# The first product of the routed expert tiles, issued in two halves of 64 tokens

## The reference: what is computed

```python
x = x + gnn(layernorm(x), adj, adj)           # adjacency normalized, two large products
h = layernorm(layernorm(x)) * gamma + beta    # (the second one inside the ffn)
sw1, sw2, ew1, ew2 = (bit_quant(w) for w in ...)   # each row: round(w / scale) in {-1, 0, 1}, times scale
shared = silu(h @ sw1.T) @ sw2.T                          # 512 -> 1024 -> 512
probs = softmax(h @ router_w.T); e = argmax(probs); gate = max(probs)
routed = gate * (silu(h @ ew1[e].T) @ ew2[e].T)           # only the expert that is chosen
out = x + shared + routed
```

## Time and profile before

| | |
|---|---|
| median of three runs | 705.73 us (703.64 to 707.68) |
| the profiled execution's own time | 702.86 us |
| its span, first to last instruction | 701.2 us |
| TensorE matmuls busy, share of the span | 648.4 us, 92% |
| TensorE weight loads busy | 381.6 us, 54% |
| DVE busy | 469.2 us, 67% |
| ACT busy | 389.6 us, 56% |
| mean granted TensorE clock | 0.991 |

### The profile page before, as it was taken

The page is one execution under the profiler, slowest core; times in us unless marked ns, Lnnn a source line. Parts: engine busy times, 40 slices in busy tenths (PEclk is TensorE's granted clock), DMA queues, the critical chain, the costliest instruction groups (busy, mean ns, idle before and its releaser), DMA issues.

```text
span 701.2 us, 15954 instructions
## 1 busy us (share of the span) xinstructions
PE 648.4 (92%) x5281; PEld 381.6 (54%) x5281; DVE 469.2 (67%) x1031; ACT 389.6 (56%) x726; POOL 151.7 (22%) x171
## 2 busy tenths in 40 slices
PE   0798999999979999999998789999999999999995
PEld 0343444444434554445434367777767677777773
DVE  4878988566664555688788669756855565555553
ACT  1658648879986776777657653333432242424241
POOL 2234430000000000012323206200021353434322
PEclk9999999999999999999999999999999999999999
DMA  8999962675897777866576896643284876868641
GB/s 348 417 421 417 421 255 62 194 196 155 237 242 251 264 259 253 282 225 237 175 270 218 241 248 166 173 111 96 76 141 131 197 195 176 187 185 181 177 141 31
DMA packets 107103, 151.68 MB, mean 216 GB/s; under 512 B 64286, under 2 KB 64286, under 8 KB 102944
## 3 DMA queue, kind: packets, MB, share of 16 engines
q1 hardware_dynamic: 91280, 117.74, 53.5%
q0 software_dynamic: 6960, 20.99, 9.9%
q10 hardware_dynamic: 8800, 12.09, 5.7%
HBM read 119.57 MB, written 19.16 MB: 198 GB/s over the span
## 4 chain that ended last, share of the span: by engine, by line
PE 54%; DMA 14%; DVE 13%; ACT 9%; issue 7%; SPq 1%; POOL 1%; DVEq 0%; ACTq 0%; POOLq 0%
PE bank L1545 16%; PE bank L1517 16%; PE bank L1390 7%; PE bank L1392 7%; PE bank L1391 7%; DMA region<-in_adj_t 6%; ACT junk L748 4%; DMA work<-in_w 3%; ACT region L760 2%; DVE work L1096 2%; DVE region L986 2%; PE bank L1421 2%; DMA work<-in_adj_t 1%; DVE region L1192 1%; DVE region L982 1%
## 5 line engine op out<-in xcount | busy, mean ns | idle before, releaser
L1545 PE MATMUL bank<-region,work 128*128 (+1 forms) x624 | 141.6, 379 | 4.4 <-DVE work L1244 4.2
L886 ACT ACTIVATE work<-work 128x512 f32<-128x512 f32 x78 | 48.5, 622 | 171.1 <-DVE work L1234 171.1
L1390 PE MATMUL bank<-zreg,work 128*128 (+1 forms) x256 | 98.2, 384 | 12.3 <-DVE work L1164 10.9
L1517 PE MATMUL bank<-zreg,region 128*128 128x128 f16 x1728 | 100.9, 219 | 0.0
L1517 PEld LDWEIGHTS bank<-zreg,region 128*128 (+1 forms) x1728 | 98.1, 98 | 4.2
L1391 PE MATMUL bank<-zreg,work 128*128 (+1 forms) x256 | 98.2, 384 | 0.0
L1392 PE MATMUL bank<-zreg,work 128*128 (+1 forms) x256 | 98.0, 383 | 0.0
L1390 PE MATMUL bank<-region,work 128*128 128x512 f16 x192 | 74.1, 386 | 25.4 <-DVE region L1010 25.4
L1545 PEld LDWEIGHTS bank<-region,work 128*128 128x128 f16 x624 | 58.9, 98 | 70.4 <-issue 7.4
L748 ACT ACTIVATE junk<-work 128x512 f16<-128x512 f32 x124 | 77.6, 625 | 15.9 <-DMA work<-in_w 13.8
L1244 DVE SCALAR_TENSOR_TENSOR work<-work 128x512 f16<-128x512 f32 x78 | 53.7, 691 | 48.8 <-ACT work L893 48.8
(11 more groups left out here) (154 smaller groups left out, 946.8 us busy)
## 6 DMA issues: line engine op xcount, KB each, us to landing
work<-in_w SPq DMA_DIRECT2D x62, 512.0 KB, 4.1
region<-in_adj SPq DMA_DIRECT2D x16, 1024.0 KB, 10.7
region<-in_adj_t SPq DMA_DIRECT2D x16, 1024.0 KB, 7.5
work<-in_adj_t SPq DMA_DIRECT2D x32, 384.0 KB, 4.4
zreg<-s_scratch SPq DMA_DIRECT2D x24, 256.0 KB, 3.9
xb<-in_w SPq DMA_DIRECT2D x10, 512.0 KB, 4.2
zreg<-in_x SPq DMA_DIRECT2D x4, 1024.0 KB, 9.7
h_scratch<-hb POOLq DMA_DIRECT2D x16, 256.0 KB, 3.4
```

The source lines that it names most:

```text
L886: nc.scalar.activation(h1[:, cols], pre[:, cols], ACT.Silu).then_inc(h1_ok, 1)
L1390: nc.tensor.matmul(dst, a_hi, b_hi, start=start, stop=False, skip_group_check=True)
L1517: last = nc.tensor.matmul(ps_h[b][f // 4][:, (f % 4) * P:(f % 4 + 1) * P], w, ht[n % RING][:, c:c + P], start=(f % 4 == 0 and d == 0 and h ...
L1545: last = nc.tensor.matmul(ps_y[b][:, :].rearrange("p (d c) -> p d c", d=DB), h1hl[:, b, h, f * P:(f + 1) * P], w, start=(f == 0 and h == 0 ...
```

## The change

For tiles from `NT` on, the 128 tokens are taken in two halves of 64 columns: for each weight square the first half's high and low part, then the second half's, so four matmuls, each with its own weight load, where there were two. `w` is still written once per square, ahead of the loops. The shared tiles keep one pass of 128 columns. The `start` flag stays on the first matmul of a bank.

```diff
                 for f in range(FB):
                     for d in range(DB):
                         w = w1t[:, ds(u * (4 * CHUNK) + (f // 2) * CHUNK + d * 2 * P + (f % 2) * P, P)]
-                        for h in range(2):
-                            c = (h * DB + d) * P
-                            last = nc.tensor.matmul(ps_h[b][f // 4][:, (f % 4) * P:(f % 4 + 1) * P], w,
-                                                    ht[n % RING][:, c:c + P], start=(f % 4 == 0 and d == 0 and h == 0),
-                                                    stop=False, skip_group_check=True)
+                        width = P if n < NT else P // 2
+                        for t in range(0, P, width):
+                            for h in range(2):
+                                c = (h * DB + d) * P + t
+                                last = nc.tensor.matmul(ps_h[b][f // 4][:, (f % 4) * P + t:(f % 4) * P + t + width], w,
+                                                        ht[n % RING][:, c:c + width],
+                                                        start=(f % 4 == 0 and d == 0 and h == 0 and t == 0),
+                                                        stop=False, skip_group_check=True)
                 last.then_inc(m1_ok, 1)
```

## The result

The changed kernel took 744.54 us (median of 4 runs, 743.23 to 745.34) beside 706.7 us for the kernel before: a ratio of 1.0546, 95% interval 1.0516 to 1.0577, **+38 us**. The forecast was +17, with 742 as the upper end of the range. The same kernel, run again on two later occasions beside the kernel before, took 721.21 us (ratio 1.0278, 1.0228 to 1.0327) and 721.99 us (1.0253, 1.0212 to 1.0294), **+19 us** each, while the kernel before took 701.92 and 702.74. The sign is the same each time, and the loss lies in the routed tiles each time, but 19 us of the first measurement belong to that occasion. Both parts have to be explained.

A forecast was written before the change was run, and what follows sets the result against it. TensorE was taken to bound the routed tiles: 0.80 us for the first product plus 0.03 for the second, times 23, is 19.1 us, less 1.8 hidden, +17.3 on 705.73, giving 723.0 us; 8-in-10 range 709 to 742.

The forecast's parts named there:

- TensorE bounds the stage: Routed tiles: TensorE sets the end, at 7.03 us a tile without idle time, so any lengthening is paid 23 times.
- The array: First product: matmuls of 64 columns cost TensorE's array 29.2 ns each, +0.16 us a tile, 3.6 us over 23 tiles.
- One address per square: First product of routed tiles: still one run-time address computation per weight square, 736 records in all.
- A queue of 32 instructions: Start of a first product: 32 queued instructions now hold four weight squares instead of eight, a lead of 0.47 us.
- The stream's step: TensorE's instruction stream, first product: 132 + 12 + 7 = 151 ns a square, against 117 for the array.
- 1.8 us hidden behind the chain at the first routed tiles: First routed tiles: TensorE's wait behind a gather, a scales transfer and DVE work absorbs 1.8 us of the loss.
- The read of the expert's number: Second product, two blocks in: stream needs 0.89 us against the array's 0.86, +0.03 us a tile.
- pauses of the stream: First product: pauses go by instructions passed, about 8 ns a square before and 15 after, +7 ns.
- (a): Rival, first product: the stream hides and the array alone pays, +1.9 us, 707.6 us; chance 0.08.
- (b): Rival, first product: the stream is dearer, 218 ns a square or a second address each, +58 us, 764; chance 0.10.
- (c): Rival: faster, if halves let the array overlap work that it does not now; chance 0.02.
- Theory G: Experiments' theory: TensorE's instructions arrive late only while GpSimd's transfers of rows are under way; e5_quiet forecast at 711 to 717 us.

The follow-up runs named there:

- e3_shared: Kernel before with the split done in the 16 shared tiles alone, routed tiles whole: 709.98 us, 1.0066 of the kernel before.
- e8_quiet_static: Changed kernel with small unindexed transfers on GpSimd's queue and a constant weight address in the first product: 703.94 us, 1.0018 of the kernel before.
- e5_quiet: Changed kernel with GpSimd's queue moving 4 to 8 elements a row, not by index, instead of gathering and scattering whole rows: 712.82 us, 1.0140 of the kernel before.
- d1_after: Changed kernel unaltered, run a third time as control on the last pair's chip: 721.99 us, 1.0253 of the kernel before.
- e6_quiet_before: Kernel before with small unindexed transfers on GpSimd's queue instead of gathers and scatters: 700.99 us, 0.9977 of the kernel before.
- d2_quiet: Changed kernel with small unindexed transfers on GpSimd's queue, on the same chip as d1_after: 714.05 us, 1.0147 of the kernel before.
- e1_even: Changed kernel with only the 12 even routed tiles split, the 11 odd ones whole: 730.72 us, 1.0379 of the kernel before.
- e2_static: Changed kernel with a constant weight address in the first product, so no address computations there: 729.26 us, 1.0357 of the kernel before.
- e4_plain: Changed kernel with the routed tiles' token loads copying without transposing: 741.75 us, 1.0496 of the kernel before.
- c1_after: Changed kernel unaltered, run again as control on the fourth occasion: 721.21 us, 1.0278 of the kernel before.

## Why the prediction was right or wrong, point by point

- **TensorE bounds the stage, and a tile's lengthening is paid 23 times.** Right: DVE, ACT and the DMAs kept their work; no new wait of theirs stands in the routed tiles.
- **The array, 29.2 ns a matmul, +0.16 us a tile.** Right: 29.1 ns in `e3_shared`, 7.19 for 7.03 us a tile in `e8_quiet_static`, in all 2.95 us for my 3.6.
- **The Trainium skill's rule** (TensorE: Matmul & The Clock Gate, section Back-to-back issue gap), columns over 2.4 GHz plus 2.5 ns: this case's rows agree, 29.1 ns at 64 columns. The section gives that rule for a matmul by itself, and about 81 ns for a load with its matmul at 128 columns; here the pairs ran at 55.9 ns, and the measurement decides. As a price of the change the rule's 3.7 us were a part of 19 to 38.
- **One address per square, 736 records.** Right, 736 after the change.
- **A queue of 32 instructions, so four squares of lead instead of eight.** Right: five addresses before the first matmul. By the Trainium skill (TensorE: Matmul & The Clock Gate, its opening table) the queue takes 64; the rows before and after both show 32.
- **The stream's step, 151 ns a square.** Wrong: 133 ns. The four added instructions cost the sequencer nothing (my 12 ns), and its pauses did not grow with the instructions passed (my 7 ns). With 133 ns my own sum gives 27 x 0.133 + 0.3 = 3.89 us for the first product, and 3.8 to 4.0 were measured, for the 4.38 that I forecast. The steady price is so 0.42 to 0.49 us a tile, not 0.83: 23 x 0.45 = 10.4 us, not 19.1. With the 1.6 us of `e5_quiet`'s three waits that makes 12.0, and 11.8 us lie between it and its control.
- **1.8 us hidden behind the chain at the first routed tiles.** Right: of the two waits behind DVE only that at the last second product is left in `d1_after` (0.4 us), and in the first measurement the early one is 0.18 us, where it was 1.1. In `e6_quiet_before`, where that chain is shorter, 1.9 us are gained, which agrees with its size.
- **The read of the expert's number, +0.03 us a tile.** Too small where GpSimd moves rows: it was taken at 0.3 us, and its median in the first measurement is 0.53, with 3.2 us of "issue" ahead of second products' matmuls in all; without the rows (`d2_quiet`) it is 0.30, with 0.3 us.
- **What was not in the sum at all: the holes.** This is the step that failed. I had written that pauses of the stream go by instructions fetched and cost a few nanoseconds each, and took the rate at which instructions reach the sequencer as given. In the kernel before no first product of the profiled execution shows a hole. With 128 loads and 128 matmuls in 3.9 us a piece of the program comes late in places and stops the array for up to 1.7 us, and in others a square takes 0.7 us and more. On the later occasions that is some 7.9 us (`d1_after` less `d2_quiet`), in the first measurement about 29 us in the routed tiles with 4 us more at the end. The low clock behind the longest holes and DVE's late start at the end are counted in these.
- **The total.** 723.0 was forecast. The 721.2 and 722.0 of the later occasions agree only because two errors nearly cancel: 6 us too much for the step (17.3 where 11.3 stay without GpSimd's rows), 8 us of holes left out. Against the first measurement the forecast was 21 us short, and that is the holes.

Of the rivals, (a) named the right fact, that added instructions cost nothing in the sequencer, but drew the wrong result, since 133 ns are above the 127 from which it decides. Of (b) there was no sign. (c) did not come.

**What stays open.** Why the holes took nearly four times as long in the first measurement, and much of that in three kernels of the first occasion after it too (`e1_even`, `e2_static`, `e4_plain`), is not shown: the chip, where memory was placed and the occasion all changed together. The long holes of the later occasions are pieces of the program that land late. For the series of holes of the first measurement it is only argued that instructions come late, from "issue" as the cause, from the sequencer having no address to show in them, and from GpSimd's transfers under way; the packets say that it is not for want of a landed piece. Theory G is shown for the later occasions; for the first one only the timelines of `e3_shared` speak for it. What starts DVE 1.3 us later in the last tile of the first measurement the profile does not name.

## What to carry to other kernels

Before splitting a matmul, count the instructions and not only the columns: the array charged 0.16 us a tile for it, the sequencer's address computations twice that once the queue's lead was cut in half, and the holes up to eight times. A stream that is already slower than the array (132 ns a square against 112 here) and lives from a lead gives no warning in the busy rows; look for the sequencer's own records and for how many of them lie ahead of the first matmul. Where "issue" stands in straight-line code, set the landings of the instruction packets beside the holes. And put the kernel itself beside its experiments each time: here 20 us of "gain" were the occasion's.

## What the runs showed of the hardware that I had not expected

- TensorE's sequencer takes 133 ns for an address computation with the loads and matmuls behind it, whether they are four or eight.
- 128 loads and 128 matmuls of 64 columns pass in 3.73 us without a hole at 471 us, and at 519 us, when GpSimd moves rows, with holes of 0.4 us, every fourth to sixth matmul (`e3_shared`). Whether the token rows are found by index or lie in order made no difference that could be told (721.21 and 719.97 us side by side).
- After a 16,384-byte packet of TensorE's instructions has landed, the matmuls that waited for it go on 1.2 to 1.6 us later (`c1_after`, `d1_after`, `d2_quiet`).
- Holes are frequent enough at times for TensorE's granted clock to fall: behind 8 us with 3.9 us of matmuls (541 to 549 us) the granted clock is 0.66 in the mean from 549.5 to 556 us, part of it at the 1.2 GHz level.
- One and the same program took 744.5, 721.2 and 722.0 us on three occasions, the kernel before 706.7, 701.9 and 702.7. A kernel that lives close to its supply of instructions is more uneven between occasions than its runs on one of them (743.2 to 745.3) let one see.
